# One product of the second convolution squared on ScalarE from a sum that DMA transfers form

## The reference

```python
x = x + _L0_conv_ref(_gn(x), w3, b3, w5, b5, wr, br)
x = x + _L1_conv_ref(_gn(x), filters)
```

```python
spot = concatenate([ones, patches(x, 3)], axis=-1)
feat = (spot[..., :, None] * spot[..., None, :]).reshape(..., M * M)
out = einsum('bcyxf,ocf->boyx', feat, filters)
```

## Time and profile before

| | |
|---|---|
| median of 3 runs | 295.14 us |
| the profiled execution: its time | 294.93 us |
| its span | 293.1 us |
| mean granted TensorE clock | 0.994 |
| TensorE matmuls busy | 271.8 us, 93% |
| VectorE busy | 253.7 us, 87% |
| ScalarE busy | 94.8 us, 32% |
| GpSimd busy | 31.0 us, 11% |
| moved by DMA | 11.45 MB, mean 39 GB/s |

### The profile page before, as it was taken

How to read it: one execution, slowest core, us unless ns; L and a number is a source line. 1 busy time by engine, 2 the same in 40 slices (tenths; PEclk the granted TensorE clock), 3 DMA queues, 4 the chain that set the end, 5 groups by cost and what they waited for, 6 DMA issues and landing times. The chain is left out here.

```text
span 293.1 us, 13502 instructions
## 1 busy us (share of the span) xinstructions
PE 271.8 (93%) x6416; PEld 127.5 (44%) x6416; DVE 253.7 (87%) x224; ACT 94.8 (32%) x137; POOL 31.0 (11%) x84
## 2 busy tenths in 40 slices
PE   0499999999989999999999999999999999998990
PEld 0133333444434443364547376444344355652640
DVE  3999799999999969797999999696999999996203
ACT  4532006999069789629400000002250000000000
POOL 5703990000110000000000000000000000000000
PEclk9999999999999999999999999999999999999997
DMA  6975000000000000000000000058000000000067
GB/s 185 374 201 119 3 2 4 2 6 2 4 0 4 4 2 2 4 2 2 6 2 4 2 4 2 2 105 188 2 4 2 2 4 2 2 4 2 17 133 143
DMA packets 19462, 11.45 MB, mean 39 GB/s; under 512 B 18000, under 2 KB 18128, under 8 KB 19280
## 3 DMA queue, kind: packets, MB, share of 16 engines
q1 hardware_dynamic: 14768, 9.06, 12.2%
q10 hardware_dynamic: 4640, 1.53, 2.3%
HBM read 6.40 MB, written 4.19 MB: 36 GB/s over the span
## 5 line engine op out<-in xcount | busy, mean ns | idle before, releaser
L1125 PE MATMUL acc<-product,weight 32*32 32x512 f32 (+1 forms) x3200 | 135.5, 604 | 1.3 <-DVE arena L881 1.1
L1125 PEld LDWEIGHTS acc<-product,weight 32*32 32x32 f32 (+1 forms) x3200 | 67.8, 110 | 64.9 <-issue 48.0
L987 DVE TENSOR_TENSOR product<-plane 128x4096 f32<-128x4096 f32 x18 | 79.0, 4429 | 0.1
L1125 PE MATMUL acc<-raw,weight 32*32 32x512 f32 (+1 forms) x736 | 34.1, 602 | 0.0
L1168 PE MATMUL acc<-product,middle 32*64 32x512 f32 (+1 forms) x576 | 29.9, 597 | 0.0
L592 ACT ACTIVATE scaled<-acc 128x2048 f32<-128x2048 f32 x2 | 3.8, 1881 | 61.9 <-PE acc L1125 61.9
L555 ACT ACTIVATE raw<-arena 32x512 f32<-32x512 f32 x32 | 21.9, 683 | 0.5
L1125 PEld LDWEIGHTS acc<-raw,weight 32*32 32x32 f32 (+1 forms) x736 | 15.2, 111 | 15.5 <-issue 12.2
L1125 PE MATMUL acc<-product,arena 32*32 32x512 f32 (+1 forms) x448 | 21.2, 604 | 0.0
L555 ACT ACTIVATE raw<-product 32x512 f32<-32x512 f32 x28 | 19.0, 679 | 2.7 <-DVE product L740 2.3
L814 DVE BATCH_NORM_STATS2 stats<-raw 128x6 f32<-128x512 f32 x32 | 19.6, 681 | 0.2
(11 more groups left out here) (139 smaller groups left out, 263.7 us busy)
## 6 DMA issues: line engine op xcount, KB each, us to landing
raw<-in_x SPq DMA_DIRECT2D x8, 512.0 KB, 8.7
out<-raw SPq DMA_DIRECT2D x16, 128.0 KB, 2.9
arena<-in_L_conv_filters SPq DMA_DIRECT2D x4, 400.0 KB, 7.1
out<-raw SPq DMA_DIRECT2D x16, 64.0 KB, 2.4
out<-raw ACTq DMA_DIRECT2D x16, 64.0 KB, 2.7
arena<-in_L_conv_w ACTq DMA_DIRECT2D x4, 100.0 KB, 4.1
w_in<-in_L_conv_w ACTq DMA_DIRECT2D x2, 36.0 KB, 1.9
w_in<-in_L_conv_w SPq DMA_DIRECT2D x2, 36.0 KB, 2.3
```

What stands on the lines that cost most here:

```text
L987: nc.vector.tensor_tensor(both_halves(g, u), plane_halves(g), plane_halves(g, PRODUCTS[k][0] * PITCH + PRODUCTS[k][1]), ALU.mult)\
L1125: return nc.tensor.matmul(acc[32 * s:32 * (s + strips), j, r, :], weights[32 * r:32 * r + 32, t:t + strips, :] .rearrange("p t c -> p (t c ...
```

## The change

Unit 13 is no longer multiplied on VectorE. With a the plane and b the plane shifted by (1, 2), ab = ((a + b)^2 - a^2 - b^2) / 2. For each group, SP copies `plane[g]` into the new tile `added_planes` in six bands of eleven rows, and GpSimd issues, for each band, a DMA that adds the shifted plane to it; each copy waits for the one before, each add for its copy and the add before. ScalarE squares the sum into unit 13's home, borders included. GpSimd halves unit 13's taps in the filters' sums and subtracts them from the square's taps. Both groups use the one tile `added_planes`; it lies over the tiles of the 3x3 weights. The home's borders are no longer zero after group 0, so GpSimd writes those of `product[0]` anew and VectorE's group 1 `LINEAR` waits for that (`borders` 7). The descriptor scratch is set to 1024 bytes per partition.

```diff
--- before.py
+++ after.py
@@ -80,6 +80,9 @@
 LINEAR, SQUARE, SQUARE_MIXED, NEXT, LINEAR_SIDES, SQUARE_SIDES, NEXT_SIDES = range(7)
 LAST_UNIT = N_PRODUCTS + 4
 FAR_ROW, DIAGONAL, DIAGONAL_SIDES = 9, 7, LAST_UNIT + 1
+ADDED = 13
+PARTS = 6
+BAND = (H + 2) // PARTS * PITCH
 
 
 UNIT_HOME = ({LINEAR: 1, SQUARE: 3, SQUARE_MIXED: 0, NEXT: 2, LINEAR_SIDES: "raw0", SQUARE_SIDES: 1,
@@ -94,10 +97,10 @@
 
 
 MADE = (["square sum", "linear cross", "square cross", "linear left", "next", "square left", "linear right",
-         "square right", 7, 8] + list(range(10, LAST_UNIT + 1)),
+         "square right", 7, 8] + [u for u in range(10, LAST_UNIT + 1) if u != ADDED],
         ["linear sum", "linear cross", "square sum", "square cross", "next", DIAGONAL, "linear left", "linear right",
          "square left", "square right", "next left", "next right", "diagonal left", "diagonal right", 8]
-        + list(range(10, LAST_UNIT + 1)))
+        + [u for u in range(10, LAST_UNIT + 1) if u != ADDED])
 UNIT_OF = {"linear": (LINEAR, LINEAR_SIDES), "square": (SQUARE_MIXED, SQUARE_SIDES), "next": (None, NEXT_SIDES),
            "diagonal": (None, DIAGONAL_SIDES)}
 
@@ -132,8 +135,9 @@
         edges = sb("edges", [128, NG, 4, W])
         arena = sb("arena", [128, FILTER_LEN + (N_WEIGHT0 + N_WEIGHT1) * C + 2 * 25 * C])
         filters_in = arena[:, 0:FILTER_LEN]
-        w3_in = sb("w3_in", [128, C * 9])
-        w3_taps = sb("w3_taps", [128, 9, C])
+        added_planes = sb("added_planes", [128, PLANE_LEN])
+        w3_in = added_planes[:, 0:C * 9]
+        w3_taps = added_planes[:, C * 9:2 * C * 9].rearrange("p (n c) -> p n c", c=C)
         scaled3 = sb("scaled3", [128, len(EY_EX), 9, C])
         at = FILTER_LEN
         folded_at = at
@@ -236,6 +240,9 @@
         stream_made = sem("stream_made")
         square_ready = sem("square_ready")
         far_row_ready = sem("far_row_ready")
+        plane_copied = sem("plane_copied")
+        planes_added = sem("planes_added")
+        added_squared = sem("added_squared")
         halved = sem("halved")
         unit_used = sem("unit_used")
         stored = sem("stored")
@@ -275,6 +282,11 @@
 
         def plane_half(g, col):
             return view(plane[g], PLANE_AT + col, (PITCH, H), (2, HALF_W))
+
+        def band(tile, n, shift=0):
+
+            at = PITCH + n * BAND + shift
+            return tile[:, at:at + BAND]
 
         def half_at(g, name):
 
@@ -368,6 +380,14 @@
             for r in range(GROUP):
                 sp.dma_start(arena[32 * r:32 * r + 32, 0:FILTER_LEN], filters.rearrange("o c i j -> o (c i j)"))\
                   .then_inc(filters_landed, 16)
+            for g in range(NG):
+                sp.wait_ge(plane_dve, NG + g + 1)
+                sp.wait_ge(plane_act, NG + g + 1)
+                if g == 1:
+                    sp.wait_ge(added_squared, 1)
+                for n in range(PARTS):
+                    sp.dma_start(band(added_planes, n), band(plane[g], n)).then_inc(plane_copied, 16)
+                    sp.wait_ge(plane_copied, 16 * (PARTS * g + n + 1))
             for r in range(GROUP):
                 sp.wait_ge(evicted, GROUP + r + 1)
                 store(sp, 0, r, range(STRIPS))
@@ -483,6 +503,12 @@
             pool.wait_ge(halved, 2)
             for a in (FIRST1[0], FIRST1[0] + 6):
                 last = nc.gpsimd.tensor_tensor(sums[:, a:a + 3, :], sums[:, a:a + 3, :], far_row, ALU.subtract)
+            last.then_inc(halved, 1)
+            added_taps = sums[:, FIRST1[ADDED - 5]:FIRST1[ADDED - 5] + 2, :]
+            nc.gpsimd.tensor_scalar(added_taps, added_taps, 0.5, None, ALU.mult).then_inc(halved, 1)
+            pool.wait_ge(halved, 4)
+            for a in (FIRST1[0], FIRST1[0] + 7):
+                last = nc.gpsimd.tensor_tensor(sums[:, a:a + 2, :], sums[:, a:a + 2, :], added_taps, ALU.subtract)
             last.then_inc(sums_ready, 1)
 
 
@@ -503,9 +529,22 @@
             pool.wait_ge(odd_spread, GROUP - 1)
             pool.wait_ge(odd_taken, 1)
             stream_borders(product[2]).then_inc(borders, 1)
+
+            def add_planes(g):
+                d = PRODUCTS[ADDED - 5]
+                for n in range(PARTS):
+                    pool.wait_ge(plane_copied, 16 * (PARTS * g + n + 1))
+                    pool.dma_start(band(added_planes, n), band(plane[g], n, d[0] * PITCH + d[1]), accum_op=ALU.add)\
+                        .then_inc(planes_added, 16)
+                    pool.wait_ge(planes_added, 16 * (PARTS * g + n + 1))
+
+            add_planes(0)
             pool.wait_ge(plane_dve, NG + 2)
             pool.wait_ge(plane_act, NG + 2)
             stream_borders(raw[1]).then_inc(borders, 1)
+            add_planes(1)
+            wait_used(pool, 0, ADDED)
+            stream_borders(home(0, ADDED)).then_inc(borders, 1)
 
             for u, before in zip(WHOLE_UNITS, (11, 12)):
                 wait_used(pool, 1, before)
@@ -610,6 +649,14 @@
                 wait_used(act, g, LINEAR_SIDES)
                 nc.scalar.activation(both_halves(g, FAR_ROW), both_halves(g, LINEAR_SIDES), ACT.Square)\
                     .then_inc(far_row_ready, 1)
+
+            def square_added(g):
+                act.wait_ge(planes_added, 16 * PARTS * (g + 1))
+                act.wait_ge(borders, (2, 6)[g])
+                wait_used(act, g, 8)
+                nc.scalar.activation(view(home(g, ADDED), 0, (HPITCH, H + 2), (HALF_LEN, 2), (1, HPITCH)),
+                                     view(added_planes, PITCH, (PITCH, H + 2), (1, 2), (2, HPITCH)), ACT.Square)\
+                    .then_inc(added_squared, 1)
 
             def scale_shifts(shifts):
                 for n in shifts:
@@ -655,10 +702,12 @@
             normalise(3)
             square_far_row(0)
             spread_offset()
+            square_added(0)
             square(1)
             keep_cross(1)
             keep_sum(1)
             square_far_row(1)
+            square_added(1)
             for block in range(2):
                 for r in range(GROUP):
                     act.wait_ge(evicted, (2 + block) * GROUP + r + 1)
@@ -939,8 +988,11 @@
                     before = {SQUARE_SIDES: LINEAR, 8: SQUARE_MIXED, 9: LINEAR_SIDES, 10: SQUARE_SIDES, 11: NEXT,
                               12: 7, 13: 8, 14: 9, 15: 10, 16: 11, 17: 12}.get(u)
                     dve.wait_ge(borders, {3: 1, 0: 2, 1: 3, "raw0": 4, 2: 5}[UNIT_HOME[g][u]])
-                elif u in (LINEAR, SQUARE_MIXED, NEXT, DIAGONAL):
-                    wait_used(dve, 0, {LINEAR: 13, SQUARE_MIXED: 15, NEXT: 16, DIAGONAL: 17}[u])
+                elif u == LINEAR:
+                    dve.wait_ge(borders, 7)
+                    before = None
+                elif u in (SQUARE_MIXED, NEXT, DIAGONAL):
+                    wait_used(dve, 0, {SQUARE_MIXED: 15, NEXT: 16, DIAGONAL: 17}[u])
                     before = None
                 else:
                     before = {LINEAR_SIDES: LINEAR, SQUARE_SIDES: SQUARE_MIXED, 10: SQUARE_SIDES, 11: NEXT_SIDES,
@@ -1085,7 +1137,7 @@
             make_offset()
             multiply(0, 10)
             mix(0)
-            for u in range(11, LAST_UNIT + 1):
+            for u in (11, 12, 14, 15, 16, 17):
                 multiply(0, u)
             dve.wait_ge(plane_act, NG + 2)
             dve.wait_ge(borders, 6)
@@ -1107,7 +1159,7 @@
             diagonal_right(1)
             multiply(1, 8)
             mix(1)
-            for u in range(10, LAST_UNIT + 1):
+            for u in (10, 11, 12, 14, 15, 16, 17):
                 multiply(1, u)
             for odd in (0, 1):
                 add_columns(odd)
@@ -1333,6 +1385,8 @@
             def wait_made(g, u):
                 if u == FAR_ROW:
                     pe.wait_ge(far_row_ready, g + 1)
+                elif u == ADDED:
+                    pe.wait_ge(added_squared, g + 1)
                 else:
                     pe.wait_ge(stream_made, made(g, "next" if u == NEXT else u))
 
@@ -1455,7 +1509,7 @@
     import concourse.bacc as bacc
     from concourse.bass_utils import run_bass_kernel_spmd
 
-    nc = bacc.Bacc("TRN2", target_bir_lowering=False, num_devices=1)
+    nc = bacc.Bacc("TRN2", target_bir_lowering=False, num_devices=1, dynamic_dma_scratch_size=1024)
     names = ("x", "L0_conv_w3", "L0_conv_b3", "L0_conv_w5", "L0_conv_b5", "L0_conv_wr", "L0_conv_br",
              "L1_conv_filters")
     arrays, args = {}, []
```

## The result

The changed kernel takes 301.61 us (median of 4 runs, 300.27 to 302.62) against 295.12 us before: 1.0206 times as long (95% interval 1.0179 to 1.0232), 6.1 us by the ratio. The forecast was 297.5 us, slower, for the reason that now shows, but with too small a size. The profiled execution took 301.88 us for a span of 300.1, 7.0 us more than the span before.

What follows compares the result with a forecast made beforehand. TensorE was taken to set the pace, except at the first add_columns. The late linear_sum(1) less the removal's gain, 182.6 - 178.9 - 1.1 = +2.6 us, on 294.93 gave 297.5 us; range 293.3 to 311.3 us.

Steps and rivals of the forecast that it cites:

- What bounds the kernel: Second convolution: TensorE sets the pace and VectorE runs ahead, except at the first add_columns, a 1.1 us wait.
- what the removal is worth: Two VectorE multiplies of 4.43 us go; only TensorE's 1.06 us wait for add_columns(0) is gained.
- Weights, scratch, both squares: GpSimd's weight work, about 1.5 us more, has 17 us of cover; ScalarE's squares have 10 and 9 us; no cost.
- fails only from a = 9.6 us: Group 0's copy and six adds, from 85.0 to 145.8 us, stay covered unless each add reaches 9.6 us.
- a: Time of one GpSimd adding DMA in a group's chain c + 6a, taken as 4.8 us.
- This is the step that decides: VectorE's linear_sum(1) waits for product[0]'s borders behind group 1's adds; shift generally 6a - 26.2, taken as +2.6 us.
- 178.9 + 1.1 = 180.0 us: Group 1 moves by t - 178.9, less the 1.06 us gained; shift taken as 182.6 - 178.9 - 1.1.
- I take 2.9 + 1.0 + 0.9: One add: plain copy 2.9, reading the destination 1.0, GpSimd's own part 0.9; 4.8 us in sum.
- t: Release of VectorE's linear_sum(1), at 150.3 + c + 6a + 0.5 + about 0.1: 182.6 us.
- c: Time of one SP band copy of 363 KB: about 1.9 us fixed plus 1.0 us for bytes, 2.9 us.
- TensorE's pause: TensorE idle once or twice between 191 and 201 us, about 3 us in sum.
- Rival (2): VectorE's multiplies hold up GpSimd's adds before 170 us; first two take 8.9 us each, 305.6 us; chance 0.06.

Runs made afterwards that it cites:

- drop_alone: The kernel before without unit 13's two multiplies, its product left out of the result: 294.22 us, 0.9952 of the kernel before.
- bf_no_chain0: The changed kernel with product[0]'s borders written before group 1's adds, and without group 0's copies and adds: 0.9963 of the kernel before.
- parts3: The changed kernel with three bands of 22 rows instead of six of 11: 1.0026 of the kernel before.
- no_copies: The changed kernel without group 1's six copies, its sum left wrong: 295.76 us, 1.0003 of the kernel before.
- bf_parts3: The changed kernel with product[0]'s borders written before group 1's adds, and three bands instead of six: 1.0042 of the kernel before.
- parts11: The changed kernel with eleven bands of six rows instead of six of eleven: 314.75 us, 1.0662 of the kernel before.

## Why the prediction was right in its mechanism and wrong in its size

- *What bounds the kernel, and what the removal is worth*: right. 1.4 us instead of 1.06 (drop_alone).
- *Weights, scratch, both squares*: right, nothing there. The second square was ready before TensorE asked.
- *Group 0's chain "fails only from a = 9.6 us"*: right for the wait, since no one waited for it, but its cost was put at nothing. The first square came at 147.04 us for 145.8 us, because TensorE was 1.1 us late by then, and every kernel with these transfers was late there (see bf_no_chain0).
- *"This is the step that decides"*: right. Moving it took back 6.5 us, lengthening it moved the end one for one, and it stops to matter where the forecast said: with `linear_sum(1)` at 180.3 us (parts3) TensorE has no pause, at 181.0 us (no_copies) one of 0.2 us, for a working that gives 178.9 + 1.1 = 180.0 us.
- *"I take 2.9 + 1.0 + 0.9": the term that was mis-sized.* t was forecast at 182.6 us and came at 186.92 us. Of the 4.3 us, 1.2 are the late square; c was 3.96 us (151.59 to 155.55 us) and not 2.9, 1.1 us; the six adds were 30.8 us (a = 5.13 us) and not 28.8 (4.8 us), 2.0 us. In the copy it wasn't the bytes: in the DMA view its bulk moved from 152.8 to 153.8 us at some 380 GB/s, the 1.0 us that was taken, and single packets followed for another 0.8 us. An add undisturbed is 4.1 us, under the 4.8 taken, of which the bulk takes 1.9 us, as the 1.0 + 1.0 us had it, and GpSimd's issue 0.86 us for the 0.9; but six in a row never were undisturbed. By 4.1 us and the old c the chain would have been hidden. So 4.8 us was near the 5.13 us partly by luck: the single add was taken too long, and what stretches adds in company was left out. In the changed kernel the four adds with copies moving or an instruction packet (last section) before or among their data took 5.0 to 6.1 us, the other two 4.2 and 4.3 us. The DMA view of the first copy, 151.5 to 155.5 us in 40 slices:

```profile
GB/s 0 0 0 0 0 164 0 0 0 0 0 0 0 348 378 436 378 407 436 378 319 348 117 0 29 0 29 29 29 0 29 29 0 0 0 0 0 0 0 0
```

- *TensorE's pause was counted once.* It costs a second time in the clock. The first half at full speed would have ended 5.9 us after 198.47, the second could start at 205.0 us when `evict(0, 1)` was through, and end at 210.9 us; it ended at 211.7 us. So of the 1.5 us that the low clock took, 0.8 us count.
- *The sum of it*: 2.6 us forecast, + 3.1 us for c and the adds, + 0.8 us for the clock, + 1.1 us late before the first square, - 0.3 us for the removal is 7.3 us; the span grew by 7.0 us. The clock and the lateness the forecast had at nothing, and the removal it took 0.3 us too small.
- Rival (2), the multiplies' lock, did not happen. Its opposite in the Trainium skill, "SBUF — State Buffer" (Who interferes with whom), which lets a two-input VectorE instruction hinder only GpSimd's reads, agrees: adds of 4.0 and 4.1 us beside such instructions. The same page's section says that DMA never contends with a compute engine; the 1.0 us that TensorE lost in bf_parts3 came after the last add's data and has no wait to show for it, so it neither bears that out nor speaks against it.
- The Trainium skill's 2.0 us and bytes at 436 GB/s ("DMA: Bandwidth & Descriptors", Anatomy of one DMA) gives an estimate of 2.85 us for an add that took 3.9 us at the least; together with the halved rate of "Collectives: The Full Stack" (The bandwidth ceiling) the estimate is 3.7 us, near it, and the bulk of an add did move at about half the rate of the copy's, 200 for 380 GB/s.

## What to carry to other kernels

Ask of every wait put on a queue what stands behind it: here a memset of 0.5 us that another engine needed stood behind 35 us of transfers that nobody needed for another 60 us, and swapping the two was worth 6.5 us. Before an engine is relieved, find the places where its time ends last: VectorE's time in group 0 was worth nothing, so buying it back with twelve transfers could not gain. A chain of dependent transfers is priced at what one takes in company, not alone, and a pause of TensorE, where the clock falls in it, at more than its length.

## What was not expected of the hardware

An add is sometimes 4 us and sometimes 5.7 us with no copy in flight. The DMA view of two adds of no_copies, over 157.5 to 161.4 us and 170.9 to 176.4 us, in 40 slices each:

```profile
GB/s 0 0 0 0 0 0 0 0 0 0 0 0 0 0 298 179 208 238 179 268 60 298 179 208 238 208 238 60 298 179 208 238 30 0 0 0 0 0 0 0
...
GB/s 0 0 0 0 0 0 0 0 0 225 211 190 127 275 169 190 190 127 275 190 169 190 148 21 0 21 0 0 21 21 0 21 21 0 21 0 0 0 0 0
q8 instruction: 1, 0.02, 2.0%
```

In both the bulk moves in 1.9 us, at some 200 GB/s. In the second, single packets follow for another 1.6 us, as if one of the 16 engines were late. In that stretch, and not in the first, lies a 16 KB packet of the instruction queue. The adds of 5.4, 4.8 and 4.6 us have such a packet in front of their data or in it, that of 3.9 us has none. That one engine's share stands behind such a packet is inferred from this coincidence; no run here put the packets elsewhere. It would also fit that parts11's last add, with TensorE standing still and no such packet, was its shortest, 3.1 us. One add does not fit well: in bf_no_chain0 that of 179.84 us had such a packet 1 us in front of its data and still took 4.2 us.

The low clock after a pause did not depend on its length here: the 256 matmuls took 13.2 us after 5.8 us and 13.3 us after 19.6 us.
